# Expert stage: routing weights spread through DRAM a run ahead, input and output turned in 32x32 squares and moved by transfers

## The reference

```python
h = _layernorm(x, axis=-1) * (1 + cb) + sb
x = x + gb * _L0_ffn_ref(h, ...)
# _L0_ffn_ref, x2 = h as (tokens, 128):
scores = sigmoid(x2 @ gate_w.T)
sc = scores + bias_e                          # choose by sc:
# the 2 best of 4 groups by the sum of each group's 2 best,
# then the 4 best experts within them -> topk_idx
topk_w = 2.5 * scores[topk_idx] / (sum + 1e-20)
combine = zeros((T, 16)).at[rows, topk_idx].add(topk_w)
for e in range(16):                           # 64 inner units each
    acc += combine[:, e, None] * (relu(x2 @ up_w[e].T) ** 2 @ down_w[e].T)
out = acc + relu(x2 @ shared_up.T) ** 2 @ shared_down.T   # 256 inner units
```

## Time and profile before

| | |
|---|---|
| median of three executions | 2152.71 us |
| profiled execution, its own time | 2151.95 us |
| span of that execution in the profile | 2150.1 us |
| TensorE busy over the span | 2047.2 us (95%) |
| VectorE, ScalarE, GpSimd busy | 1650.3, 1438.3, 618.3 us |
| granted TensorE clock, mean | 0.98 |
| all DMA, mean rate over the span | 16 GB/s |

### The profile page before, as it was taken

The page is one execution under the profiler, slowest core; times in us unless marked ns, Lnnn a source line. Parts: engine busy times, 40 slices in busy tenths (PEclk is TensorE's granted clock), DMA queues, the critical chain, the costliest instruction groups (busy, mean ns, idle before and its releaser), DMA issues. The chain is left out here.

```text
span 2150.1 us, 40463 instructions
## 1 busy us (share of the span) xinstructions
PE 2047.2 (95%) x14885; PEld 1372.3 (64%) x14885; DVE 1650.3 (77%) x4015; ACT 1438.3 (67%) x1931; POOL 618.3 (29%) x862
## 2 busy tenths in 40 slices
PE   3899999999999999997999999799999996999998
PEld 1577777777777777775444444577777773444443
DVE  3888888888888888874566665577777776999997
ACT  1687877778887777873666666466666663555554
POOL 1345444544544454552000000133333331000000
PEclk9999999999999999997999999899999997999999
DMA  5000000000000000001000000000000000000000
GB/s 165 21 21 21 21 11 21 21 21 21 21 21 11 21 21 21 21 21 55 1 0 1 1 1 1 1 2 2 2 2 2 2 2 1 10 16 11 15 11 20
DMA packets 32834, 35.30 MB, mean 16 GB/s; under 512 B 6864, under 2 KB 26496, under 8 KB 32640
## 3 DMA queue, kind: packets, MB, share of 16 engines
q1 hardware_dynamic: 32640, 32.73, 5.8%
HBM read 11.75 MB, written 4.19 MB: 7 GB/s over the span
## 5 line engine op out<-in xcount | busy, mean ns | idle before, releaser
L864 POOL TENSOR_SCALAR_AFFINE_SELECT pr<-pr 128x512 f32<-128x512 f32 x256 | 202.2, 813 | 370.7 <-ACT pr L795 370.7
L422 PE MATMUL a_pO<-va,pr 128*128 128x66 f32 x2048 | 304.6, 272 | 1.9 <-POOL pr L864 1.5
L422 PEld LDWEIGHTS a_pO<-va,pr 128*128 128x128 f32 x2048 | 273.7, 193 | 18.9 <-issue 15.4
L1628 ACT ACTIVATE c_pr<-c_pS 128x1536 f32<-128x1536 f32 x128 | 186.0, 1453 | 119.3 <-PE c_pS L1440 119.3
L1683 POOL TENSOR_SCALAR_AFFINE_SELECT c_pr<-c_pr 128x512 f32<-128x512 f32 x256 | 158.0, 641 | 265.4 <-DVE c_pr L1548 265.4
L761 ACT ACTIVATE sq<-a_pW 128x512 f32<-128x512 f32 x192 | 114.4, 597 | 145.4 <-PE a_pW L363 142.7
L789 ACT ACTIVATE th<-a_pS 128x1536 f32<-128x1536 f32 x128 | 185.9, 1453 | 30.1 <-PE a_pS L407 29.6
L423 PE MATMUL a_pO<-va,pr 128*128 128x66 f32 x1024 | 199.0, 276 | 0.0
L795 ACT ACTIVATE pr<-th 128x1536 f32<-128x1536 f32 x128 | 190.5, 1488 | 3.1
L407 PE MATMUL a_pS<-qs,k 128*128 128x512 f16 (+1 forms) x1024 | 187.3, 326 | 0.9 <-issue 0.9
L1548 DVE TENSOR_SCALAR c_pr<-c_pr 128x1536 f32<-128x1536 f32 x128 | 122.6, 958 | 78.4 <-ACT c_pr L1628 78.4
(11 more groups left out here) (259 smaller groups left out, 4509.1 us busy)
## 6 DMA issues: line engine op xcount, KB each, us to landing
k<-k SPq DMA_DIRECT2D x64, 256.0 KB, 3.6
x<-in_L_attn_tokens_dram SPq DMA_DIRECT2D x8, 512.0 KB, 6.8
out_dram<-x SPq DMA_DIRECT2D x16, 256.0 KB, 2.3
d_h<-in_L_ffn_h_w_dram SPq DMA_DIRECT2D x2, 1024.0 KB, 7.4
wmod<-in_L_wmod_dram SPq DMA_DIRECT2D x2, 384.0 KB, 4.0
d_w<-in_L_ffn_w_w_dram SPq DMA_DIRECT2D x3, 256.0 KB, 3.2
a_wq<-in_L_attn_Wq_dram SPq DMA_DIRECT2D x1, 512.0 KB, 7.1
a_wkv<-in_L_attn_Wkv_dram SPq DMA_DIRECT2D x1, 512.0 KB, 6.9
```

The lines of the kernel that those rows point to most:

```text
L422: pe.matmul(out, w[:, hh * N + t * P:hh * N + (t + 1) * P], v[:, 0, p, :], start=True, stop=t == 0)
L864: last = gp.affine_select(out=part, in_=part, compare_op=ALU.is_ge, fill=0.0, base=0, pattern=[[0, HPG], [1, P]], channel_multiplier=-1)
L1628: act.activation(pr[g][:, :, :], pS[:, :, 0:N + P], ACT.Exp, scale=float(1.0 / np.sqrt(np.float32(DQ)))).then_inc(s_ex, 1)
```

## The change

TensorE's turns and spreads leave the stage. VectorE turns in blocks of 32x32 (`dve.transpose`), and transfers on the sync queue carry the blocks to their places: 16 transfers of 32 partitions x 512 bytes for the input of a run, 16 for its output. The weights are turned the same way, written to a DRAM buffer `b_by_expert` in four transfers, and read back in eight, each of which repeats each of two experts' 2 KB rows over 64 partitions. `dve_weigh` multiplies by that SBUF tile. Input and routing run two iterations ahead of the products instead of one, `hT` has three buffers, `pU` four, `s` two; the float16 pair of the weights becomes one float32. The order of VectorE and of the sync queue is new.

```diff
+        xn, xt, xh, og, ot, out = (sb(x, [P, S4, T4, SQ]) for x in ('xn', 'xt', 'xh', 'og', 'ot', 'out'))
+        cwp, cwT = (sb(x, [P, T4, SQ]) for x in ('cwp', 'cwT'))
+        cwB = [sb(f'cwB{k}', [P, RT, W]) for k in range(2)]
+        by_expert = nc.dram_tensor('b_by_expert', (E, T4, P // SQ, SQ), F32, kind='Internal').ap()
...
+        def sp_move_in(sp, n):
+            sp.wait_ge(s_xt, n + 1)
+            if n >= 1:
+                sp.wait_ge(s_hT, n)
+            for j in range(S4):
+                for g in range(S4):
+                    sp.dma_start(xh[SQ * g:SQ * (g + 1), j, :, :], xt[SQ * j:SQ * (j + 1), g, :, :]).then_inc(s_xh, 16)
+
+        def sp_move_out(sp, n):
+            sp.wait_ge(s_ot, n + 1)
+            if n >= 1:
+                sp.wait_ge(s_st, ADD_STEPS * (n - 1) + 1)
+            for j in range(S4):
+                for g in range(S4):
+                    sp.dma_start(out[SQ * j:SQ * (j + 1), g, :, :], ot[SQ * g:SQ * (g + 1), j, :, :]).then_inc(s_out, 16)
+
+        def sp_spread(sp, n):
+            sp.wait_ge(s_cT, n + 1)
+            if n >= 1:
+                for j in range(RT):
+                    sp.wait_ge(s_cw[j], 16 * n)
+            for j in range(S4):
+                sp.dma_start(by_expert[:, :, j, :], cwT[SQ * j:SQ * j + E, :, :]).then_inc(s_cd, 16)
+            sp.wait_ge(s_cd, 16 * S4 * (n + 1))
+            if n >= 2:
+                sp.wait_ge(s_a, RT * (n - 1))
+            rows = by_expert.rearrange('(j y) t k r -> j y (t k r)', y=2)
+            for j in range(RT):
+                sp.dma_start(cwB[n % 2][:, j, :], rows[j].unsqueeze(1).broadcast_to((2, EI, W))).then_inc(s_cw[j], 16)
+
         @block.sync
         def _(sp):
+            for n in range(2):
+                sp_move_in(sp, n)
             ahead(sp)
+            for n in range(-1, RUNS + 1):
+                if 0 <= n + 1 < RUNS:
+                    sp_spread(sp, n + 1)
+                if 0 <= n - 1 < RUNS:
+                    sp_move_out(sp, n - 1)
+                if 0 <= n + 3 < RUNS:
+                    sp_move_in(sp, n + 3)
...
-                    pe_turn_weights(pe, n)
...
-                    pe_spread(pe, n, 2)
...
-                    pe_front(pe, n + 1)
...
-                    pe_back(pe, n - 1)
...
         def dve_normalise(dve, n):
             if n >= 1:
-                dve.wait_ge(s_xT, n)
+                dve.wait_ge(s_xt, n)
...
+            dve.wait_ge(s_xn, n + 1)
+            if n >= 1:
+                dve.wait_ge(s_xh, 16 * S4 * S4 * n)
+            dve.transpose(xt[:, :, :, :].rearrange('p g t r -> p (g t r)'), xn[:, :, :, :].rearrange('p g t s -> p (g t s)')).then_inc(s_xt, 1)
...
             if n >= 1:
-                dve.wait_ge(s_cT, n)
-            dve.tensor_copy(cwp[:, :, 0:E], cw[:, :, :]).then_inc(s_rt, 1)
-            dve.wait_ge(s_rt, base + 31)
-            dve.tensor_tensor(cwp[:, :, E:2 * E], cw[:, :, :], cwp[:, :, 0:E], ALU.subtract).then_inc(s_rt, 1)
+                dve.wait_ge(s_cd, 16 * S4 * n)
+            dve.transpose(cwT[:, :, :].rearrange('p t r -> p (t r)'), cwp[:, :, :].rearrange('p t e -> p (t e)')).then_inc(s_cT, 1)
...
-            dve.wait_ge(s_cb, RT * n + j + 1)
+            dve.wait_ge(s_cw[j], 16 * (n + 1))
...
-            dve.tensor_tensor(a[(IT * n + u) % 4][:, :], q[j % 4][:, :], pC[j % 2][:, :], ALU.mult).then_inc(s_a, 1)
+            dve.tensor_tensor(a[(IT * n + u) % 4][:, :], q[j % 4][:, :], cwB[n % 2][:, j, :], ALU.mult).then_inc(s_a, 1)
...
+        def dve_turn_out(dve, n):
+            dve.wait_ge(s_og, n + 1)
+            if n >= 1:
+                dve.wait_ge(s_out, 16 * S4 * S4 * n)
+            dve.transpose(ot[:, :, :, :].rearrange('p j t s -> p (j t s)'), og[:, :, :, :].rearrange('p j t r -> p (j t r)')).then_inc(s_ot, 1)
...
         def dve_add(dve, n):
-            dve.wait_ge(s_oT, n + 1)
-            add_to_x(dve, c, s_st, n, T4, pB[:, :])
+            dve.wait_ge(s_out, 16 * S4 * S4 * (n + 1))
+            xt4 = c.x[:, n * T4:(n + 1) * T4, :].rearrange('p t (g s) -> p t g s', s=SQ)
+            dve.tensor_tensor(xt4, xt4, out[:, :, :, :].rearrange('p g t s -> p t g s'), ALU.add).then_inc(s_st, 1)
...
         def act_modulate(act, n):
-            if n >= 2:
-                act.wait_ge(s_up, IT * (n - 1))
-            act.wait_ge(s_xT, n + 1)
+            if n >= 3:
+                act.wait_ge(s_up, IT * (n - 2))
+            act.wait_ge(s_xh, 16 * S4 * S4 * (n + 1))
...
-                    act_take_weights(act, n)
```

More of the change, by code:

```diff
@@ L952, in moe @@
         uT, dT, gT = (sb('uT', [D, IT * P]), sb('dT', [P, IT * D]), sb('gT', [D, E]))
-        sel = sb('sel', [P, RT, P], F16)
         lt4 = sb('lt4', [P, NG, NG])
-        xn = sb('xn', [P, T4, D])
-        hT = [sb(f'hT{k}', [D, W]) for k in range(2)]
-        s, cw = (sb(x, [P, T4, E]) for x in ('s', 'cw'))
+        S4 = P // SQ
+        xn, xt, xh, og, ot, out = (sb(x, [P, S4, T4, SQ]) for x in ('xn', 'xt', 'xh', 'og', 'ot', 'out'))
+        hT = [sb(f'hT{k}', [D, W]) for k in range(3)]
+        s = [sb(f's{k}', [P, T4, E]) for k in range(2)]
+        cw = sb('cw', [P, T4, E])
         sc, mk, rep = (sb(x, [P, T4, ROW]) for x in ('sc', 'mk', 'rep'))
@@ L1002, in pe_route @@
             if n >= 1:
-                pe.wait_ge(s_cw, n)
+                pe.wait_ge(s_ex, n)
             for t in range(T4):
-                last = pe.matmul(pR[:, t * E:(t + 1) * E], hT[n % 2][:, t * P:(t + 1) * P], gT[:, :], start=True, stop=True)
+                last = pe.matmul(pR[:, t * E:(t + 1) * E], hT[n % 3][:, t * P:(t + 1) * P], gT[:, :], start=True, stop=True)
             last.then_inc(s_lg, 1)
[L1008 to L1013, removed]
         def pe_up(pe, n, u):
@@ L1017, in pe_up @@
                 pe.wait_ge(s_hT, n + 1)
-            if n or u >= 2:
-                pe.wait_ge(s_r, IT * n + u - 1)
+            if n or u >= 4:
+                pe.wait_ge(s_r, IT * n + u - 3)
             t = weights_of(u)
[L1021 to L1029, removed]
+            pe.matmul(pU[(IT * n + u) % 4][:, :], uT[:, t * P:(t + 1) * P], hT[n % 3][:, :], start=True, stop=True).then_inc(s_up, 1)
         def pe_down(pe, n, u):
@@ L1039, in pe_down @@
             pe.matmul(pD[:, :], dT[:, t * D:(t + 1) * D], a[(IT * n + u) % 4][:, :], start=u == 0, stop=u == IT - 1).then_inc(s_dn, 1)
[L1041 to L1047, removed]
         @block.tensor
@@ L1061, in _ @@
             pe.wait_ge(s_taken, len(turns))
-            pe.wait_ge(s_k, 4)
-            for n in range(-1, RUNS + 1):
+            for n in range(-2, RUNS + 1):
                 if 0 <= n < RUNS:
@@ L1102, in dve_normalise @@
             if n >= 1:
[L1103 removed]
+                dve.wait_ge(s_xt, n)
             for t in range(T4):
[L1105 removed]
+                i = n * T4 + t
+                last = dve.tensor_scalar(xn[:, :, t, :], c.x[:, i, :].rearrange('p (g s) -> p g s', s=SQ), c.mv[:, i, 0:1],
+                                         c.rs[:, i:i + 1], ALU.subtract, ALU.mult)
             last.then_inc(s_xn, 1)
+            dve.wait_ge(s_xn, n + 1)
+            if n >= 1:
+                dve.wait_ge(s_xh, 16 * S4 * S4 * n)
+            dve.transpose(xt[:, :, :, :].rearrange('p g t r -> p (g t r)'), xn[:, :, :, :].rearrange('p g t s -> p (g t s)')).then_inc(s_xt, 1)
         def dve_scores(dve, n):
@@ L1203, in _ @@
             dve.wait_ge(s_km, 4)
-            for n in range(-1, RUNS + 1):
+            dve_normalise(dve, 0)
+            dve_normalise(dve, 1)
+            for n in range(-2, RUNS + 1):
                 if 0 <= n - 1 < RUNS:
                     dve_weigh(dve, n - 1, 9)
-                if 0 <= n < RUNS:
-                    dve_weights(dve, n)
                 if 0 <= n + 1 < RUNS:
-                    dve_normalise(dve, n + 1)
+                    dve_weights(dve, n + 1)
                 if 0 <= n < RUNS:
@@ L1213, in _ @@
                     dve_weigh(dve, n, 3)
+                if 0 <= n - 1 < RUNS:
+                    dve_turn_out(dve, n - 1)
+                if 0 <= n < RUNS:
                     dve_weigh(dve, n, 4)
+                    dve_weigh(dve, n, 5)
+                if 0 <= n + 2 < RUNS:
+                    dve_scores(dve, n + 2)
+                if 0 <= n < RUNS:
+                    dve_weigh(dve, n, 6)
+                if 0 <= n + 2 < RUNS:
+                    dve_groups(dve, n + 2)
                 if 0 <= n - 1 < RUNS:
@@ L1301, in _ @@
                     act_relu(act, n, 3)
-                if 0 <= n + 1 < RUNS:
-                    act_modulate(act, n + 1)
+                if 0 <= n + 2 < RUNS:
+                    act_modulate(act, n + 2)
                 if 0 <= n < RUNS:
@@ L1318, in _ @@
         def _(gp):
-            gp.memset(sel[:, :, :], 0.0).then_inc(s_k, 1)
             gp.memset(lt4[:, :, :], 1.0).then_inc(s_k, 1)
-            for k in range(2):
-                gp.wait_ge(s_k, 2 + k)
-                m = sel[:, :, :].rearrange('r t (x i) -> r t x i', i=EI)
```

(2 more changed lines are left out.)

95 lines of the change are left out of this document (34 added, 61 removed).

## The result

The changed kernel takes 2915.57 us (median of four executions, 2913.35 to 2916.52) against 2152.65 us before: a ratio of 1.3543 with a 95% interval of 1.3519 to 1.3566. The profiled execution took 2916.52 us, 764.6 more than the one before. All of that is in the expert stage: its last copy of statistics now ends at 2121.8, before at 1357.4, 764.4 later.

The account below looks back on a forecast made before the run. Before, TensorE bound the kernel at 20.94 us per run; after, serial sync-queue transfers and VectorE work would, at 3.5 + 49.1 + 7.7 + 7.5 = 67.8 us. With start and end, 2152 + 758 = 2910 us, range 2320 to 3000.

Parts of the forecast that it names:

- two engines: Broadcast loads with leading count 2: each is carried by 2 engines, 46 us for eight; chance 0.70, range 2766 to 2996.
- the ring: Sync queue and VectorE: writes, loads with moves out, VectorE's rest and moves in follow serially without overlap, 67.8 us a period.
- the packet: Broadcast loads: one 2 KB packet takes 90 ns on its engine, with 72 and 96 as the ends.
- the issue: Sync queue: each of 44 transfers per run costs 0.47 us to issue, with 0.60 kept as the upper value.
- the number of periods: Expert stage: 13 full periods of 67.8 us after the first spreads, putting the last spread at 2022.
- TensorE's gain: TensorE in the expert stage: removed spreads and turns save 2.9 us per run, leaving 18.1; 46 us over 16 runs.
- VectorE's transposes: VectorE's new block transposes: 0.69 us taken, with 0.3 and 1.4 as the ends; VectorE's work per run becomes about 15 us.
- Start and end: Expert stage's edges: first spread works from about 1037, last spread at 2022, stage ends at 2116.
- Sixteen engines: Rival for the broadcast loads: all 16 engines carry them, period 31.7 us, total 2340 us; chance 0.22, range 2310 to 2420.
- The case in which the moves don't stand behind the loads: Rival on the sync queue: moves out land beneath the loads, period about 54 us, total 2730 us; chance 0.05.
- TensorE as the bound: Rival: the sync queue costs little, needing issues below 0.16 us; 46 us saved, total 2137 us; chance 0.03.
- The clock: TensorE in the expert stage: busy about a quarter, its granted clock at or near 0.50 for much of it.

Follow-up runs that it names:

- The last version: Changed kernel with TensorE's turns of input and output kept, weights through DRAM, loads cut by a leading count of 64: 2126.67 us, ratio 0.9868 against the original kernel.
- wide loads: Changed kernel with its eight broadcast loads cut to one expert's 64 partitions and two tiles each, leading count 64 instead of 2: 2432.0 us.
- the version through DRAM: Reordered kernel with leading-count-64 loads, each turn's sixteen moves replaced by one DRAM write and four reads, four 512 KB loads: 2238.33 us; loads issued last: 2181.70 us.

## Why the prediction was right

The forecast was 2910 us; 2915.6 were measured, inside the 2766 to 2996 that the prediction gave for two engines. The step that decided, two engines for a load and the ring around it, is right and shown. That the number is so close is partly luck, as the packet, the issue and the number of periods show. Point by point:

- **TensorE's gain.** Not visible in the changed kernel, where TensorE waits. The last version shows it: it drops the spreads and the turning of the weights (1.75 + 0.27) and its period is 1.98 us shorter.
- **VectorE's transposes.** 0.70 us for 128x512 and 0.31 for 128x128 were measured, 0.69 taken.
- **Two engines.** Right, the step that decided: 2 small packets per load, 13.1% of the engines' time and 51 GB/s; 4, 26.1% and 102 for a leading count of 4. The rule that the Trainium skill gives in "DMA: Bandwidth & Descriptors", section "Why a DMA increments its semaphore by 16 and not by 1", holds here for 2, 4 and 64 on the sync queue. From GpSimd's queue the same load with its leading count of 2 had 16 small packets.
- **The packet.** 90 ns were taken, 80 measured, so the 512 packets of an engine are 41.1 us instead of 46. The 3.1 us that the prediction added for the first packet and the moves' share are 5.8, so the whole term, put at 49.1, is 46.9. The bound of 96 came from all sixteen engines together; two alone are faster.
- **The issue.** 0.47 us were taken for a move, 0.63 measured (10.00 us for 16), a little above the 0.60 kept as the bound. Moves in cost 10.3 instead of 7.5. So the period of 68.2 against 67.8 owes much to luck: the packets were 5 us too long, what follows them and the moves in 2.8 us too short each, VectorE 0.5 too long, the writes 0.2 too short.
- **The ring.** Writes 3.7 against 3.5, VectorE 7.2 against 7.7. The add's wait, the wait of the queue in front of the moves in, and the order in which they follow are as told. The wait of 9.05 us that ScalarE's modulation brings to a product ends at 1832.52, and the output is turned 30 us before its moves are issued, so that wait costs the ring nothing, as told. The queue's order as the reason for the late moves is shown by issuing them elsewhere. Not as told is where they wait. The prediction had the loads issued in 3.8 us and the moves in the two engines' rings behind them. In the trace the issuing itself is held up: the first move is issued 30.3 us after the first load, the last issue ends at 1878.44, and the add starts 2.1 us after that, the time in which a small transfer lands. So most of the wait lies in front of the issue; what the rings added to it can't be told apart here.
- **Start and end.** First spread at 1040.8 (1037), the last at 2025.4 (2022), the end at 2121.8 (2116). The prediction counted 13 full periods. There are 12, of 68.8 us in the mean, 12 us more than twelve of 67.8; the thirteenth distance, 1967.10 to 2025.43, has no input left to move and is 58.3 us, 9.5 less. These two errors nearly cancel as well.
- **The rivals.** Sixteen engines: 2340 were forecast, 2432 measured with wide loads. The difference is the issue, 32 moves, writes and loads all nearer 0.63 than 0.47: period 37.7 instead of 31.7. The thirteen distances took 485 us instead of 412, 73 us of the 92. The case in which the moves don't stand behind the loads was put at 54 us a period and 2730, and came out at 49.3 and 2649. TensorE as the bound: excluded by the issue, 0.63 us where less than 0.16 was needed.
- **The clock.** The page shows 6 tenths in the stage; in the stretch of 1866 to 1878, in which TensorE does nothing, it is 0.50, the 1.2 GHz level. It costs the ring nothing, since none of its waits is ended by TensorE.

What stays open: why the wide loads run at 210 to 250 GB/s where the earlier trace rows had 361 (they fill 64 partitions each and read the same rows again and again, and no run separates the two), and whether a second DRAM buffer would bring the version through DRAM to TensorE's 18.1 us.

## What to carry to other kernels

Read the access pattern of a transfer before its bytes: a leading count of 2 made 2 MB per run take 41 us, and the same bytes in the same number of transfers with a leading count of 64 took 9. A queue is an order: what is short and waited for goes in front of what is long and needed a run later, or on another queue. Count the issues against the run that is to hide them (44 x 0.63 = 27.7 is more than the 20.9 us of a run), and take off the bound engine what costs few transfers, not all that can be moved.

## What the runs showed that was not expected

- Issuing itself can be slow: a two-engine load occupies the sync queue for up to 7.88 us (median 5.01, about what 256 KB take at 51 GB/s, shortest 0.52), where eight sixteen-engine loads take 5.17 us together. Everything behind such a load waits with it.
- The same load from GpSimd's queue was cut into 512-byte packets with 16 small ones, and landed in 11.9 us (median).
- A 16 KB move between SBUF partitions costs 0.63 us of the queue when issued in a row, more than the 0.47 of small loads from DRAM, and lands in 1.8 us.
- Loads of 64 partitions each on sixteen engines reach 210 to 250 GB/s, 13 to 16 per engine, against 25.5 per engine with two or four.
